# Norms of k from rounded high and low parts, and their place behind one output product

## The chip, the cores and the metric

The kernel runs on one core of one Trainium2 chip. The metric is the device time of one execution in microseconds; lower is better. The engines are PE (TensorE), DVE (VectorE), ACT (ScalarE), POOL (GpSimd) and SP, the queue that issues the DMAs.

## The reference

The input is x of 8 batch elements, 512 tokens and 256 channels, in float32. One attention layer with 16 heads and complex q, k and v (64 real and 64 imaginary parts a head) is followed by a small feed-forward layer; each has a normalisation before and after and a residual. The change is in the norms of k:

```python
qr = q * phase[None]
kr = k * phase[None]
s = jnp.einsum('bihd,bjhd->bhij', qr, jnp.conj(kr)).real
qn = (q.real ** 2 + q.imag ** 2).sum(-1).transpose(0, 2, 1)
kn = (k.real ** 2 + k.imag ** 2).sum(-1).transpose(0, 2, 1)
maha = jnp.maximum(qn[..., None] + (E * E)[None] * kn[:, :, None, :] - 2.0 * E[None] * s, 0.0) / V[None]
logits = coef * jnp.log1p(maha / nu[None, :, None, None]) - 0.5 * DH_ * jnp.log(V)[None]
A = jax.nn.softmax(logits, axis=-1)
y = jnp.concatenate([out.real.reshape(B_, N_, DKt), out.imag.reshape(B_, N_, DKt)], axis=-1)
return y @ Wo
```

## The kernel before

The 16 heads are taken in 8 groups of two, and within a group the 8 batch elements one after the other: 64 turns, t = 0 to 63. A turn handles the pair (group, element) c; at the same time it finishes the pair before (cp) and starts the next (cn). The order on every engine is written out by hand in a function `body`, one for each engine, and semaphores with fixed counts tie the engines together.

For the next pair a turn does this. PE projects q (z = 0) and k (z = 1) into the two PSUM banks pa0 (real parts) and pa1 (imaginary parts), in `project` (L767), from weights and x that are split into a rounded high part and a low part of type float32r. ACT squares each bank (`square`, L1182). DVE multiplies the banks with the cosine and the sine (`rotate`, L1508): four products RC, IS, RS and IC for q, and four for k. POOL adds the squares of the real and the imaginary parts (`sum_squares`, L584) and combines the rotated products into qk (`rotated`, L592). The norms of k are then matrix products of the sums with a matrix of ones (`norms_k`, L778, one product for each head, on 64 rows each, float32), written into pa0 and pa1. They may begin once the last `rotate` of k has read the banks (wait on mul_dve). ACT copies them with a bias into kn (`keep_norm_k`, L1188), and POOL makes ek from kn (`decay_norm`, L602). The norms of q (`norm_q`, L786) go into pa0 and wait for the first of these copies.

Scores are a product of qk (`scores`, L807), which DVE turns into lg in two steps (`decay`, L1622, and `distance`, L1632) and, after a logarithm on ACT (L1199), a third one (`logits`, L1639). After the exponential (L1207) PE transposes the probabilities (`turn`, L819) into pp0 or pp1, ACT copies them out (L1214), and `attend` (L831) multiplies them with the values. `values` (L797) writes pp0 and pp1 too, and ACT copies these into vt (`keep_values`, L1193). `keep_y` (L1220) copies the result of a head.

The output products of the pair before are four calls of `out_project` (L842) for each turn: head 0 half 0, head 0 half 1, head 1 half 0, head 1 half 1. Each fills the whole bank po with four matmul records, and before the next may begin DVE must have read po, in `add_output` (L1660, and L1658 in the first group). This is the wait at the head of `out_project`:

```python
if half == 0:
    pe.wait_ge(y_act, c[2] + hh + 1)
pe.wait_ge(acc_dve, c[4] + 2 * hh + half)
```

So the product of head 1 half 0 waits until both halves of head 0 are added. On PE the end of a turn is: `out_project` (0,1), `turn` (0,0), `norms_k`, `out_project` (1,0), `scores` (0,0) of the next pair, `norm_q`, `scores` (0,1), `out_project` (1,1), `turn` (0,1), `scores` (0,2). On DVE the same stretch is: the rotations RS and IC of k, `add_output` (0,1), `decay` (1,3), `distance` (1,3), `add_output` (1,0), `decay` (0,0) of the next pair.

Of the kernel before, what the change touches and what calls it, by code (L numbers as in the profile page):

```python
# [21 lines left out]
F32 = mybir.dt.float32  # L22
F32R = mybir.dt.float32r
I32 = mybir.dt.int32
ALU = mybir.AluOpType
ACT = mybir.ActivationFunctionType
# [6 lines left out]
B, N, D = 8, 512, 256  # L33
H, DH = 16, 64
DK = H * DH
HID = 768
P = 128
KT = D // P
NT = N // P
HH = 2  # L40
# [24 lines left out]
def build(nc, x_d, wq_d, wk_d, wv_d, wo_d, omega_d, raw_d, tau_d, wg_d, wu_d, wd_d, out_d):  # L65
    ctx = ExitStack()
    with ctx:
# [3 lines left out]
        def sem(name):  # L71
            return ctx.enter_context(nc.semaphore(name))
# [19 lines left out]
        sq = sb("sq", [P, 2, 2, N])  # L92
# [7 lines left out]
        hx = sb("hx", [P, 4, N], F32R)  # L100
# [4 lines left out]
        heads = sb("heads", [P, HH, P])  # L105
# [72 lines left out]
        pa = [bank("pa0"), bank("pa1")]  # L178
# [45 lines left out]
        x_out = [sem(f"x_out{i}") for i in range(XBUF)]  # L224
# [5 lines left out]
        nk_rdy = sem("nk_rdy")  # L230
        nq_rdy = sem("nq_rdy")
        v_rdy = sem("v_rdy")
# [2 lines left out]
        av_rdy = sem("av_rdy")  # L235
        o_rdy = sem("o_rdy")
        sq_act = sem("sq_act")
        kn_act = sem("kn_act")
        v_act = sem("v_act")
        ln_act = sem("ln_act")  # L240
# [10 lines left out]
        sum_pool = sem("sum_pool")  # L251
# [76 lines left out]
        def width(n):  # L328
            return (TILES[n] + 1) * P

        def at(n):

            o = sum(width(k) for k in range(n))
            return slice(o, o + width(n))

        PARTS = ((0, 0), (0, 1), (1, 0))

# [382 lines left out]
        def _(pe):  # L720
            credit(pe, (proj, 4), (nk_rdy, 1), (nq_rdy, 1), (v_rdy, 2), (s_rdy, 8), (tr_rdy, 8), (av_rdy, 8), (o_rdy, 4))
            mm = pe.matmul
# [46 lines left out]
                        n += 1  # L769
                last.then_inc(proj, 1)  # L770

            def norms_k(c):

                pe.wait_ge(sum_pool, c[2] + 2)
                pe.wait_ge(mul_dve, c[8] + 8)
                for hh in range(HH):
                    row = slice(hh * DH, (hh + 1) * DH)
                    last = mm(pa[hh][:, :], heads[row, hh, :], sq[row, 1, 0, :], start=True, stop=True)  # L778
                last.then_inc(nk_rdy, 1)

            def norm_q(c):
# [53 lines left out]
            def out_project(c, par, hh, half):  # L835
# [4 lines that stand above are left out]
                for jj in range(2):  # L840
                    j = 2 * half + jj
                    last = mm(po[:, jj * D:(jj + 1) * D], yt[:, hh, j * P:(j + 1) * P], wot[:, par, hh * D:(hh + 1) * D],  # L842
                              start=True, stop=True)
                last.then_inc(o_rdy, 1)
# [69 lines left out]
            def body(it):  # L914


                c = counts(pe, it.t, PERS)
                cp, cn = previous(c), following(c)
                old, nxt = it.before is not None, it.behind is not None
                half = it.half + it.slot  # L920
                if it.opens is not None:
                    pe.wait_ge(w_lo, 3 * KT * (it.opens + 1))
                    pe.wait_ge(wo_in[it.behind], 32 * (it.opens // 2 + 1))
                if nxt:
                    project(cn, it.behind, 1 - it.slot, it.xn, half, it.own, 0, 0)
                if it.own == 1:
                    ffn_turn(2)
                if old:
                    turn(cp, 0, 2)
                scores(c, 0, 3)  # L930
                if it.own is not None and it.own < B - 1:
                    x_turn(cp, it.own + 1, 0)
                if nxt:
                    project(cn, it.behind, 1 - it.slot, it.xn, half, it.own, 0, 1)
                if old:
                    attend(cp, 0, 0, 1 - it.slot)
                    attend(cp, 0, 1, 1 - it.slot)
                    turn(cp, 0, 3)
                scores(c, 1, 0)
                if it.own is not None and it.own < B - 1:  # L940
                    x_turn(cp, it.own + 1, 1)
                if old:
                    turn(cp, 1, 0)
                    attend(cp, 0, 2, 1 - it.slot)
                if nxt:
                    project(cn, it.behind, 1 - it.slot, it.xn, half, it.own, 1, 0)
                if it.own == 1:
                    ffn_turn(3)
                    ffn_turn(4)
                    ffn_turn(5)  # L950
                if old:
                    attend(cp, 0, 3, 1 - it.slot)
                scores(c, 1, 1)
                if old:
                    turn(cp, 1, 1)
                    turn(cp, 1, 2)
                    attend(cp, 1, 0, 1 - it.slot)
                scores(c, 1, 2)
                if old:
                    turn(cp, 1, 3)  # L960
                scores(c, 1, 3)
                if it.own is not None and it.own < B - 1:
                    pe.wait_ge(x_lo, 2 * it.own + 4)
                if old:
                    out_project(cp, it.before, 0, 0)
                if nxt:
                    project(cn, it.behind, 1 - it.slot, it.xn, half, it.own, 1, 1)
                else:
                    f_transposes(0)
                if it.own == 1:  # L970
                    ffn_turn(6)
                    ffn_turn(7)
                    ffn_turn(8)
                    pe.wait_ge(ffn_ev, 9)
                if old:
                    attend(cp, 1, 1, 1 - it.slot)
                    attend(cp, 1, 2, 1 - it.slot)
                values(c, it.par, it.x, 0)
                values(c, it.par, it.x, 1)
                if old:  # L980
                    attend(cp, 1, 3, 1 - it.slot)
                    out_project(cp, it.before, 0, 1)
                turn(c, 0, 0)
                if nxt:
                    norms_k(cn)
                if old:
                    out_project(cp, it.before, 1, 0)
                if nxt:
                    scores(cn, 0, 0)
                    norm_q(cn)  # L990
                    scores(cn, 0, 1)
                if old:
                    out_project(cp, it.before, 1, 1)
                turn(c, 0, 1)
                if nxt:
                    scores(cn, 0, 2)
                else:
                    gate_up(0, 0)
                    gate_up(0, 1)
# [49 lines left out]
            c = counts(pe, G * B - 1, PERS)  # L1049
# [40 lines left out]
        def _(act):  # L1090
# [10 lines left out]
            for h in range(HH):  # L1101
                for a in range(2):
                    row = slice(h * DH + a * DH // 2, h * DH + (a + 1) * DH // 2)
# [80 lines left out]
            def keep_norm_k(c, par, hh):  # L1184
# [2 lines left out]
                act.wait_ge(ek_pool, c[8] + 4 * hh + 4 - 8)  # L1187
                act.activation(kn[:, hh, :], pa[hh][:, :], ACT.Identity, bias=ncog[:, par, 1, hh:hh + 1]).then_inc(kn_act, 1)  # L1188

            def keep_values(c, slot, half):  # L1190

                act.wait_ge(v_rdy, c[2] + 1 + half)
                act.activation(vt[:, slot, 2 * half:2 * half + 2, :].rearrange("p a n -> p (a n)"), pp[half][:, :],  # L1193
                               ACT.Copy).then_inc(v_act, 1)
# [6 lines left out]
            def exp(c, hh, n):  # L1201
                m, q = 4 * hh + n, NT * hh + TILES[n]
                act.wait_ge(f_dve, c[8] + m + 1)
                act.wait_ge(tr_rdy, c[8] + m + 1 - 8)
                if n == 0:
                    act.wait_ge(rd_dve, c[2] + hh + 1 - 2)
                act.activation(pr[:, hh, at(n)], lg[:, hh, at(n)], ACT.Exp, bias=nmax[:, q:q + 1], scale=-1.0,  # L1207
                               accum_out=den[:, q:q + 1]).then_inc(ex_act, 1)
# [56 lines left out]
            def body(it):  # L1265
# [60 lines left out]
                if not nxt:  # L1326
                    f_high(0)
                exp(c, 0, 0)
                keep_values(c, it.slot, 0)
                if old:  # L1330
                    keep_y(cp, 1)
# [100 lines left out]
        def _(dve):  # L1432
# [69 lines left out]
            def rotate(c, par, z, m):  # L1502

                r = m in (IS, IC)
                dve.wait_ge(sq_act, c[4] + 2 * z + r + 1)
                for h in range(HH):
                    dve.wait_ge(rot_pool[h], c[4] + (1 + (m in (RS, IC)) if z else 0))
                tt(rm[:, m, :], pa[r][:, :], ropet(par, m in (IS, RS)), ALU.mult).then_inc(mul_dve, 1)  # L1508
# [126 lines left out]
            def logits(c, hh, n, par):  # L1635
# [3 lines left out]
                dve.tensor_tensor_reduce(lg[:, hh, at(n)], lg[:, hh, at(n)], tab(par, hh, T3_T, w), ncog[:, par, 0, hh:hh + 1],  # L1639
                                         3e38, ALU.add, ALU.min, nmax[:, q:q + 1]).then_inc(f_dve, 1)  # L1640

            def inverse(c, hh):

                dve.wait_ge(ex_act, c[8] + 4 * hh + 4)
                rec(rden[:, NT * hh:NT * hh + NT], den[:, NT * hh:NT * hh + NT]).then_inc(rd_dve, 1)
# [111 lines left out]
            def body(it):  # L1757
# [69 lines left out]
                if nxt:  # L1827
                    rotate(cn, it.behind, 1, RS)
                    rotate(cn, it.behind, 1, IC)
                if old:  # L1830
                    add_output(cp, it.b_before, it.over, 0, 1)
                if nxt:
# [117 lines left out]
```

## Time and profile before

| | |
|---|---|
| median of 3 runs | 1871.65 us (1870.67 to 1872.46) |
| the profiled execution | 1871.72 us, of which the span from the first to the last instruction is 1869.9 us |
| mean granted TensorE clock | 0.991 |
| PE busy | 1795.5 us, 96% of the span |
| DVE, ACT, POOL busy | 87%, 84%, 79% |
| DMA | mean 63 GB/s |

Busy time is the time in which an engine had an instruction in flight, as a share of the span. Matmuls are pipelined: a matmul's row tells when it began and how long it was in flight, and the next one often begins while it still runs. What a group of matmuls takes from PE is therefore read from its start to the start of the next group.

### The profile page before, as it was taken

The page shows a single profiled execution, that of the slowest core. Times are in us where ns is not written, and L with a number is a line of the kernel's source. Part 1 is how long each engine was busy: PE and PEld are TensorE (multiplying, and loading weights), DVE is VectorE, ACT ScalarE, POOL GpSimd, SP SyncE. Part 2 cuts the span into 40 slices and gives each one's busy share as a digit, 9 for nine tenths or more (in the row PEclk, how much of TensorE's full clock was granted, in tenths as well). Part 3 has the DMA queues.
Part 4 walks back from the last instruction along what each step waited for, and adds up shares of the span by engine and source line. Part 5 has one row for each costly group of instructions (what it writes and reads, how often), then busy time and mean ns, then how long its engine had stood idle before and what let it go on. Part 6 is the DMA issues. An engine that isn't in the chain of part 4 may idle for free.

```text
span 1869.9 us, 35435 instructions
## 1 busy us (share of the span) xinstructions
PE 1795.5 (96%) x10690; PEld 1475.9 (79%) x10690; DVE 1631.4 (87%) x3852; ACT 1576.7 (84%) x3255; POOL 1470.0 (79%) x1291
## 2 busy tenths in 40 slices
PE   5799999999999999999999999999999999988997
PEld 3577788878888888778888888788888888867876
DVE  7799989989888899988898899888898888986885
ACT  5798888898888888998888888988888888876654
POOL 5677888878888888888888888888888888862664
PEclk9899999999999999999999999999999999999999
DMA  6311211131112201131203111120112111010111
GB/s 184 118 68 46 85 46 68 45 104 46 63 52 68 86 26 67 46 125 46 68 30 101 46 63 52 63 98 33 69 46 91 46 46 45 25 57 13 46 46 45
DMA packets 61100, 117.77 MB, mean 63 GB/s; under 512 B 13504, under 2 KB 42944, under 8 KB 52720
## 3 DMA queue, kind: packets, MB, share of 16 engines
q1 hardware_dynamic: 60528, 115.51, 18.4%
q8 instruction: 88, 1.44, 0.3%
q14 instruction: 100, 0.82, 0.2%
q10 hardware_dynamic: 384, 0.00, 0.0%
HBM read 99.64 MB, written 21.36 MB: 65 GB/s over the span
## 4 chain that ended last, share of the span: by engine, by line
PE 70%; DVE 11%; ACT 4%; issue 3%; POOL 2%; DMA 0%; DVEq 0%; POOLq 0%; ACTq 0%; SPq 0%
PE pa L767 15%; PE py L831 13%; PE ps L807 12%; PE po L842 10%; PE pp L797 8%; PE pp L819 6%; PE pa L778 3%; PE pa L786 2%; DVE lg L1639 2%; DVE stats L1666 1%; DVE rm L1508 1%; DVE lg L1632 1%; DVE acc L1688 1%; DVE ps L1622 1%; DVE tabs L1753 1%
## 5 line engine op out<-in xcount | busy, mean ns | idle before, releaser
L592 POOL TENSOR_TENSOR qk<-rm 64x512 f32<-64x512 f32 x504 | 697.4, 1384 | 93.7 <-PE ps L807 49.8
L602 POOL TENSOR_TENSOR ek<-tabs,kn 128x512 f32<-128x512 f32 (+3 forms) x512 | 463.7, 911 | 133.9 <-DVE lg L1632 107.0
L1639 DVE CUSTOM_DVE_ANT_0 lg<-lg,tabs,ncog 128x512 f32<-128x512 f32 (+3 forms) x512 | 445.5, 888 | 0.0
L767 PE MATMUL pa<-xt,wt 128*128 128x512 f32 x1488 | 420.8, 418 | 6.3 <-DVE rm L1514 3.7
L1508 DVE TENSOR_TENSOR rm<-pa,tabs 128x512 f32<-128x512 f32 x504 | 327.0, 676 | 75.1 <-POOL qk L592 66.1
L807 PE MATMUL ps<-qk 128*128 128x512 f32 (+3 forms) x1024 | 366.9, 443 | 12.0 <-DVE lg L1632 11.8
L831 PE MATMUL py<-pt,vt 128*128 128x128 f32 x2560 | 348.2, 275 | 0.8 <-ACT pt L1214 0.5
L1632 DVE CUSTOM_DVE_ANT_0 lg<-ps,ek,qb 128x512 f32<-128x512 f32 (+3 forms) x512 | 279.0, 545 | 76.1 <-issue 58.0
L831 PEld LDWEIGHTS py<-pt,vt 128*128 128x128 f32 x2560 | 331.1, 192 | 16.8 <-ACT pt L1214 0.7
L767 PEld LDWEIGHTS pa<-xt,wt 128*128 128x128 f32 x1488 | 273.5, 191 | 58.7 <-issue 7.9
L1199 ACT ACTIVATE lg<-lg,qb 128x512 f32<-128x512 f32 (+3 forms) x512 | 273.0, 557 | 17.4 <-DVE lg L1632 13.5
L1207 ACT ACTIVATE pr<-lg,nmax 128x512 f32<-128x512 f32 (+3 forms) x512 | 283.7, 555 | 1.5
L842 PE MATMUL po<-wot,yt 128*128 128x256 f32 x1024 | 270.4, 387 | 3.0 <-DVE acc L1660 3.0
L1214 ACT ACTIVATE pt<-pp 128x512 f32<-128x512 f32 (+3 forms) x512 | 219.8, 429 | 59.5 <-PE pp L819 42.9
L1622 DVE TENSOR_TENSOR ps<-ps,tabs 128x512 f32<-128x512 f32 (+3 forms) x512 | 249.3, 487 | 17.8 <-PE ps L807 17.6
L842 PEld LDWEIGHTS po<-wot,yt 128*128 128x128 f32 x1024 | 179.1, 190 | 81.2 <-issue 48.4
L819 PEld LDWEIGHTS pp<-ident,pr 128*128 128x128 f32 x1280 | 162.9, 141 | 92.9 <-issue 58.4
L819 PE MATMUL pp<-ident,pr 128*128 128x128 f32 x1280 | 214.3, 274 | 15.4 <-ACT pt L1214 12.8
L1660 DVE SCALAR_TENSOR_TENSOR acc<-po,rden,acc 128x256 f32<-128x256 f32 x480 | 207.6, 472 | 10.0 <-PE po L842 9.6
L1182 ACT ACTIVATE sq<-pa 128x512 f32<-128x512 f32 x256 | 151.9, 594 | 60.8 <-PE pa L767 60.6
L797 PE MATMUL pp<-wt,xt 128*128 128x256 f32 x1488 | 193.6, 286 | 0.7 <-ACT wut L1162 0.7
L584 POOL TENSOR_TENSOR sq<-sq 128x512 f32<-128x512 f32 x126 | 161.8, 1284 | 39.9 <-ACT sq L1182 39.3
(205 smaller groups left out, 2251.5 us busy)
## 6 DMA issues: line engine op xcount, KB each, us to landing
xt<-xs_d SPq DMA_DIRECT2D x56, 1024.0 KB, 4.8
tabs<-vec_d SPq DMA_DIRECT2D x7, 1536.0 KB, 6.5
xs_d<-xt SPq DMA_DIRECT2D x6, 1024.0 KB, 4.3
wt<-wraw_d SPq DMA_DIRECT2D x7, 768.0 KB, 6.7
acc<-in_L_attn_x SPq DMA_DIRECT2D x8, 512.0 KB, 6.2
tabs<-in_L_attn_x SPq DMA_DIRECT2D x8, 512.0 KB, 4.8
tabs<-rope_d SPq DMA_DIRECT2D x56, 64.0 KB, 5.8
out<-tabs SPq DMA_DIRECT2D x7, 512.0 KB, 3.2
```

The costliest lines, as they stand in the source:

```text
L592: pool.tensor_tensor(qk[part * DH:(part + 1) * DH, z * HH + hh, :], rm[row, 2 * part, :], rm[row, 2 * part + 1, :], ALU.add if part else A ...
L602: pool.tensor_tensor(ek[:, n % 2, 0:w], tab(par, hh, E2_T, w), kn[:, hh, 0:w], ALU.mult).then_inc(ek_pool, 1)
L767: last = mm(pa[r][:, :], wproj(par, z, kt, a, r * P, (r + 1) * P), xbuf[x][:, kt, b, :], start=(n == 0), stop=(n == 3 * KT - 1))
L797: last = mm(pp[half][:, jj * W2:(jj + 1) * W2], xbuf[x][:, kt, a, j * P:(j + 1) * P], wproj(par, 2, kt, b, 0, W2), start=(n == 0), stop=(n ...
L807: mm(ps[n % 2][:, 0:w], qk[:, hh, TILES[n] * P:(TILES[n] + 1) * P], qk[:, HH + hh, 0:w], start=True, stop=True).then_inc(s_rdy, 1)
L819: last = pe.transpose(pp[i][:, j * P:(j + 1) * P], pr[:, hh, o:o + P], ident[:, :])
L831: last = mm(py[:, I * P:(I + 1) * P], vt[:, slot, j, hh * P:(hh + 1) * P], pt[:, i, j * P:(j + 1) * P], start=(j == 0), stop=(j == I))
L842: last = mm(po[:, jj * D:(jj + 1) * D], yt[:, hh, j * P:(j + 1) * P], wot[:, par, hh * D:(hh + 1) * D], start=True, stop=True)
L1207: act.activation(pr[:, hh, at(n)], lg[:, hh, at(n)], ACT.Exp, bias=nmax[:, q:q + 1], scale=-1.0, accum_out=den[:, q:q + 1]).then_inc(ex_ac ...
L1508: tt(rm[:, m, :], pa[r][:, :], ropet(par, m in (IS, RS)), ALU.mult).then_inc(mul_dve, 1)
L1632: dve._custom_dve(bass.dve_ops.TENSOR_ADD_SAT, out=lg[:, hh, at(n)], in0=ps[n % 2][:, 0:w], in1=ek[:, n % 2, 0:w], s0=3e38, s1=qb[:, slot, ...
L1639: dve.tensor_tensor_reduce(lg[:, hh, at(n)], lg[:, hh, at(n)], tab(par, hh, T3_T, w), ncog[:, par, 0, hh:hh + 1], 3e38, ALU.add, ALU.min, ...
```

## The change

The norms of k are computed in another way for every pair from the second group on (t of the pair at least 8, 56 of the 63 calls in the turns). ACT writes a copy of the sums of squares, rounded to float32r, into the buffer hx (`high_sum`); DVE subtracts it from the sums to give the low part (`low_sum`); and PE makes four float32r products, high and low part for each head, in place of two float32 products. hx was a buffer for x in the first group and is free afterwards. The matrix of ones is copied once into hx as float32r. The copy on ACT stands between `exp` (0,0) and `keep_values` of half 0; the subtraction on DVE between the rotation IC of k and `add_output` (0,1). On PE `norms_k` moves behind `out_project` (1,0), in all turns, those of the first group too.

```diff
+        def parted(t):
+            return B <= t
+        def k_sums(a):
+            return hx[:, a, :]
+        round_heads = hx[:, 2, 0:HH * P].rearrange("p (h n) -> p h n", h=HH)
...
-            def norms_k(c):
+            def norms_k(c, t):
                 pe.wait_ge(sum_pool, c[2] + 2)
                 pe.wait_ge(mul_dve, c[8] + 8)
-                for hh in range(HH):
-                    row = slice(hh * DH, (hh + 1) * DH)
-                    last = mm(pa[hh][:, :], heads[row, hh, :], sq[row, 1, 0, :], start=True, stop=True)
+                if parted(t):
+                    pe.wait_ge(nl_dve, t - B + 1)
+                    for a in range(2):
+                        for hh in range(HH):
+                            row = slice(hh * DH, (hh + 1) * DH)
+                            last = mm(pa[hh][:, :], round_heads[row, hh, :], hx[row, a, :], start=(a == 0), stop=(a == 1))
+                else:
+                    for hh in range(HH):
+                        row = slice(hh * DH, (hh + 1) * DH)
+                        last = mm(pa[hh][:, :], heads[row, hh, :], sq[row, 1, 0, :], start=True, stop=True)
                 last.then_inc(nk_rdy, 1)
...
                 turn(c, 0, 0)
-                if nxt:
-                    norms_k(cn)
                 if old:
                     out_project(cp, it.before, 1, 0)
+                if nxt:
+                    norms_k(cn, it.t + 1)
                 if nxt:
                     scores(cn, 0, 0)
                     norm_q(cn)
...
+            def high_sum(t):
+                act.wait_ge(sum_pool, 2 * t + 4)
+                if t == B:
+                    act.wait_ge(v_rdy, 2 * (B - 2) + 2)
+                    act.wait_ge(x_out[2], 16 * 2)
+                    act.activation(round_heads, heads[:, :, :], ACT.Copy)
+                else:
+                    act.wait_ge(nk_rdy, t + 1)
+                act.activation(k_sums(0), sq[:, 1, 0, :], ACT.Copy).then_inc(nh_act, 1)
...
                 exp(c, 0, 0)
+                if nxt and parted(it.t + 1):
+                    high_sum(it.t + 1)
                 keep_values(c, it.slot, 0)
...
+            def low_sum(t):
+                dve.wait_ge(nh_act, t - B + 1)
+                tt(k_sums(1), sq[:, 1, 0, :], k_sums(0).bitcast(F32), ALU.subtract).then_inc(nl_dve, 1)
...
                 if nxt:
                     rotate(cn, it.behind, 1, RS)
                     rotate(cn, it.behind, 1, IC)
+                if nxt and parted(it.t + 1):
+                    low_sum(it.t + 1)
                 if old:
                     add_output(cp, it.b_before, it.over, 0, 1)
```

## Rows read from the trace of the kernel before

**Rows 1.** Two turns by engine: busy us (instructions) on each engine, clock.

```profile
core 0: us, PE busy (x) PEld busy (x) DVE busy (x) ACT busy (x) POOL busy (x), PEclk, DMA share, GB/s
270.87:295.97 25.10, 25.07 (x152) 20.76 (x153) 22.41 (x53) 22.12 (x47) 20.96 (x18) 1.00 0.12 41
905.68:930.78 25.10, 25.07 (x152) 20.77 (x153) 22.43 (x53) 22.44 (x48) 21.53 (x20) 1.00 0.22 74
```

**Rows 2.** Timeline of a middle turn: start, us, engine, line, tiles [idle before, releaser].

```profile
922.60 0.39 PE L807 MATMUL ps<-qk 128*128 128x128 f32 x2
...
923.16 2.65 POOL L592 TENSOR_TENSOR qk<-rm 64x512 f32<-64x512 f32 x2 [0.77 <-PE ps L807]
...
924.56 0.69 DVE L1508 TENSOR_TENSOR rm<-pa,tabs 128x512 f32<-128x512 f32 x1 [1.27 <-POOL qk L592]
...
927.39 3.18 POOL L592 TENSOR_TENSOR qk<-rm 64x512 f32<-64x512 f32 x2
...
927.88 1.54 DVE L1639 CUSTOM_DVE_ANT_0 lg<-lg,tabs,ncog 128x384 f32<-128x384 f32 x1
...
928.98 0.58 ACT L1193 ACTIVATE vt<-pp 128x512 f32<-128x512 f32 x1
...
929.36 1.28 DVE L1508 TENSOR_TENSOR rm<-pa,tabs 128x512 f32<-128x512 f32 x2
...
930.16 0.60 PE L819 MATMUL pp<-ident,pr 128*128 128x128 f32 x4
...
930.56 0.86 DVE L1660 SCALAR_TENSOR_TENSOR acc<-po,rden,acc 128x256 f32<-128x256 f32 x2
...
930.78 1.26 POOL L592 TENSOR_TENSOR qk<-rm 64x512 f32<-64x512 f32 x1 [0.21 <-DVE rm L1508]
930.78 1.13 PE L778 MATMUL pa<-sq,heads 64*128 64x512 f32 x4
...
931.84 1.13 PE L842 MATMUL po<-wot,yt 128*128 128x256 f32 x4
931.95 0.69 ACT L1188 ACTIVATE kn<-pa,ncog 128x512 f32<-128x512 f32 x1 [0.78 <-PE pa L778]
...
932.81 1.02 PE L807 MATMUL ps<-qk 128*128 128x512 f32 x2
...
933.67 0.95 PE L786 MATMUL pa<-heads,sq 128*128 128x2 f32 x8
...
936.40 0.58 ACT L1214 ACTIVATE pt<-pp 128x512 f32<-128x512 f32 x1
...
937.99 0.37 PEld L819 LDWEIGHTS pp<-ident,pr 128*128 128x128 f32 x2
...
938.57 1.64 PE L767 MATMUL pa<-xt,wt 128*128 128x512 f32 x6
...
940.05 1.72 PE L831 MATMUL py<-pt,vt 128*128 128x128 f32 x14
```

**Rows 3.** Timelines of PE and DVE in turn 0, an early and a late turn.

```profile
73.13 1.13 PE L807 MATMUL ps<-qk 128*128 128x512 f32 x2
...
74.09 0.50 PE L786 MATMUL pa<-heads,sq 128*128 128x2 f32 x4
...
191.60 1.28 DVE L1508 TENSOR_TENSOR rm<-pa,tabs 128x512 f32<-128x512 f32 x2
...
193.03 1.13 PE L778 MATMUL pa<-sq,heads 64*128 64x512 f32 x4 [0.46 <-DVE rm L1508]
...
1610.65 1.28 DVE L1508 TENSOR_TENSOR rm<-pa,tabs 128x512 f32<-128x512 f32 x2
...
1612.08 1.13 PE L778 MATMUL pa<-sq,heads 64*128 64x512 f32 x4
```

**Rows 4.** Groups of like instructions: count, busy us, mean ns of one, idle before.

```profile
L1721 DVE TENSOR_TENSOR tabs<-tabs,acc 128x1024 f32<-128x1024 f32 x7 | 8.8, 1260 | 1.6 <-ACT tabs L1259 1.6
L1251 ACT ACTIVATE wt<-tabs 128x512 fp32r<-128x512 f32 x36 | 22.7, 630 | 37.2 <-DVE tabs L1753 34.0 <-PE po L893 3.2
```

More of the change, by code:

```diff
@@ L237, in build @@
         sq_act = sem("sq_act")
+        nh_act = sem("nh_act")
+        nl_dve = sem("nl_dve")
         kn_act = sem("kn_act")
```

## The prediction

> **What bounds the kernel now.** I read the table of busy time by stage first, then the timeline of a middle turn on all engines, then the same place in other turns. The table shows a turn of 25.10 us in which PE is busy for 25.07 [rows 1]. The easy reading is that PE is the bound and that every microsecond of matmul removed is gained. But busy counts a matmul that is in flight, also over a short stall, and the timeline says more. The next thing to look at is what ends just before `norms_k` starts. DVE's last two rotations of k (RS, IC) run from 929.36 to 930.64, and `norms_k` begins at 930.78, 0.14 us later, while the four transposes before it, from 930.16, are in flight for 0.60 in all, so that the last has left by 930.76 and PE could take the next product at about 930.60 [rows 2]. An early turn has 191.60 + 1.28 = 192.88 and 193.03, 0.15 later, with the wait for the rotation named; a late one has 1611.93 and 1612.08, again 0.15 [rows 3]. A distance that doesn't move over the whole kernel is a wait, not a coincidence. So PE is held here by DVE, for at most 0.2 us a turn, and the loop that sets the turn is: `scores` (1,3) on PE at 922.60, POOL's rotated products that may start only after it (0.77 us idle, released by L807), DVE's rotation RC that may start only after those (1.27 us idle, released by POOL), DVE without a gap until IC ends at 930.64, then `norms_k`, and from there PE without a gap until the next `scores` (1,3) [rows 2]. In this loop PE has up to 0.2 us of slack on the way to `norms_k`, and DVE has none.
>
> **The change, part by part.** Times are those of the middle turn [rows 2].
>
> *The move on PE.* Today `norms_k` (930.78 to 931.84, 1.06 us) stands between `turn` (0,0) and `out_project` (1,0). That product waits for `add_output` (0,1), since all four output products share the bank po. The addition ends at 930.56 + 0.86 = 931.42, under `norms_k`: its cover costs nothing today. Moved behind the product, `norms_k` no longer covers it. PE would be free at 930.60 and wait.
>
> *The subtraction on DVE.* `low_sum` stands ahead of just this addition. A rotation of the same 512 columns takes 0.60 us from start to start (929.36, 930.56, two of them). Its inputs are both in SBUF; the nearest such row is the addition of 1024 columns at 1260 ns [rows 4], half of it 0.63. I take 0.61. It goes ahead of the addition in DVE's order, so the addition ends at 931.42 + 0.61 = 932.03. From the end on DVE to the start on PE I take the 0.14 of IC to `norms_k`: `out_project` (1,0) starts at 932.17 in place of 931.84, 0.33 later. Bounds: the subtraction can't be free, since its place is on the loop; the hand-over could be 0.05 to 0.2.
>
> *The norms as rounded products.* Their cost isn't in the trace. Before: four records of 64 rows, 1.06 us together. After: four float32r matmuls of 64 rows and 512 columns. A float32r matmul of 512 columns and 128 rows goes at (940.05 - 938.57)/6 = 0.247 us [rows 2]. If the two heads run side by side on their halves of the rows, as the float32 ones do (four records in 1.06 us, while two records of full height and 512 columns, `scores`, take 0.86), the four take 2 x 0.25 and 0.05 for the change of shape, 0.55. If they run one after the other, 4 x 0.25 = 1.0. I take 0.55; nothing in the program separates the two cases other than the type. Before them I allow 0.05.
>
> *What follows.* `out_project` itself takes 932.81 - 931.84 = 0.97. So `scores` (0,0) starts at 932.17 + 0.97 + 0.05 + 0.55 = 933.74 in place of 932.81, 0.93 later. Then `norm_q`, which waits for ACT's copy of the first head's norms. That copy starts today 0.11 after the next product on PE (931.95) and takes 0.69, and `scores` (0,0) needs 0.86: after the move it is the only cover. Turn 0 has just this order, and there `scores` to `norm_q` is 74.09 - 73.13 = 0.96 [rows 3], 0.10 more than the 0.86. Sum of a turn: +1.03 us.
>
> *The copy on ACT.* `high_sum` costs about 0.60 (a copy to float32r of 512 columns has 630 ns [rows 4]). It pushes `keep_values` from 928.98 to 929.6, ending 930.2, so `turn` (0,0) starts perhaps 0.1 late; that lies under PE's new wait until 932.17. If that wait weren't there it would cost about 0.1 a turn. Further on, ACT's copy of the norms comes at about 933.9 in place of 931.95, 1.9 later, where PE is 1.03 later. The copy L1214 at 936.40 then ends near 938.9 and PE's transposes need it at 937.99 + 1.03 = 939.0. That just fits, so I put nothing for it, and up to 0.2 a turn for the upper end. POOL's rotated product at 930.78 comes behind `low_sum` and moves by some 0.4; the bit of ek for (1,3) behind it isn't waited for by PE in this stretch.
>
> *The port.* Rows show that a DVE instruction that reads two tiles of SBUF stands still while POOL works: `logits` on 384 columns takes 1.54 us from 927.88, with POOL's products running from 927.39 to 930.57 at 1.59 each, so the first of them ends at about 929.0, and 929.0 + 0.4 is where DVE ends [rows 2]. The Trainium skill has the rule in "SBUF — State Buffer", section "Who interferes with whom": two SBUF inputs on DVE and a GpSimd instruction that reads SBUF exclude each other, and whoever issues first keeps the port for the whole instruction. By that rule the trace agrees. For the sum it matters who is first: `low_sum` would start at 930.56, when POOL's products have just ended (930.57), and the next one starts at 930.78, 0.22 behind. So DVE is first and POOL waits.
>
> *The first group.* In turns 1 to 6 only the order changes: the addition ends at 931.42, the product starts at 931.56, `norms_k` at 932.58 with its old 1.06, `scores` at 933.64, +0.83, and +0.10 for `norm_q`: 0.93.
>
> *The sum.* 56 turns x 1.03 = 57.7, 6 x 0.93 = 5.6, together 63. Nothing gives it back: after `scores` (0,0) PE runs without a gap to `scores` (1,3), and the chain by POOL and DVE hangs on that one. The profiled execution's own 1871.72 + 63.3 = 1935.0; it lies 0.07 from the median, so this stands for the median as well.
>
> **Rivals.**
> 1. *The chain holds, sizes at the low end.* Hand-over 0.05, no allowance before the norms, nothing for `norm_q`, order of 0.75 a turn: 42 + 4.5, 1918. If `low_sum` were hidden too (DVE finding the time in an earlier wait) the product would start at 931.56 and the turn would be +0.43: 24 + 5 = 29, 1901. Against it: there is no DVE wait between 924.56 and 930.64.
> 2. *The rounded products don't run side by side.* +0.45 a turn, 25 more: 1960. For it: no 64-row float32r matmul is in the trace.
> 3. *`low_sum` loses the port to POOL.* If POOL's product started first, DVE would stand for most of its 1.26 us: about +1.1 a turn, 62 more, 1997. It decides at 0.2 us between the two starts. The page "SBUF — State Buffer" would allow this outcome as well, since by its rule issue order alone decides.
> 4. *PE was the bound after all (the other side).* If the addition were ready when PE has finished `turn` (0,0), the whole saving of 1.06 - 0.55 = 0.5 would come through: 56 x 0.5 = 28, 1843. For this DVE's chain would have to run 1.4 us earlier against PE (932.03 against 930.60). Only 0.77 and 1.27 us of waits lie in it, and both hang on PE's own `scores` (1,3), so they don't give way. For it speaks only the busy share of PE.
> 5. *No difference*: needs the stalls to be just half as large as read, with no mechanism behind it.
>
> **How the numbers follow.** The forecast 1935 has 0.60, its own range 1915 to 1955; rival 1 in its lower part 0.10; rival 2 with 0.13; rival 3 with 0.05; rival 4 with 0.08; rival 5 with 0.04. The range for 8 in 10 takes in the lower case of rival 1 in good part and rival 2: 1908 to 1965. About 0.2% (3.7 us) is what this measurement can tell from no change. Slower 0.89, same 0.03, faster 0.08.
>
> **What the profile after would show.** PE idle before the first matmul of `out_project` (1,0), about 1.3 us a turn, released by the addition on DVE; that addition starting 0.6 us later after IC than before; the turn at about 26.1 us; the norms' four records in 0.55 us (right) or 1.0 (rival 2); `low_sum` at 0.6 us (right) or near 1.7 (rival 3); and `norm_q` 0.9 to 1.0 us behind the start of `scores` (0,0). The forecast is wrong if the additions come at the same time after `scores` (1,3) as before with `low_sum` in front of them, or if PE shows no wait at this place.

## The result

The changed kernel takes 1951.49 us (median; before 1871.16 in the same runs), a ratio of 1.0431 with the 95% interval [1.0418, 1.0443]. That is 80 us more; the forecast was 63 more, 1935, and its range ended at 1965. The profiled execution has a span of 1948.5 us, 78.6 more than before. One of the ten executions of e5 below took 9955 us and is left out of its ratio; the executions of every other kernel lie within 0.6% of each other.

First the page of the changed kernel, its busy times and its chain:

```profile
PE 1794.6 (92%) x10690; PEld 1463.7 (75%) x10690; DVE 1668.3 (86%) x3908; ACT 1590.0 (82%) x3312; POOL 1487.2 (76%) x1291
...
PE 44%; DVE 29%; issue 7%; POOL 5%; ACT 4%; DVEq 1%; POOLq 0%; DMA 0%; ACTq 0%; SPq 0%
```

PE's busy time hardly moved (1795.5 before, 1794.6 now), though the norms' matmuls now take 0.66 us to the next product and not 1.06: busy counts what is in flight, so a short wait behind a matmul that is still in flight is in it. What changed is the share, 96% before and 92% now, and the chain, in which DVE now has 29% where it had 11%. The table of busy time by stage, for a plain turn and for two turns in which ACT also computes sines for a rotation table (they are named below):

```profile
core 0: us, PE busy (x) PEld busy (x) DVE busy (x) ACT busy (x) POOL busy (x), PEclk, DMA share, GB/s
918.59:944.89 26.30, 24.98 (x154) 20.51 (x154) 23.00 (x54) 22.45 (x47) 21.27 (x18) 1.00 0.11 40
410.62:439.42 28.80, 25.37 (x153) 20.42 (x153) 22.77 (x54) 25.07 (x51) 21.78 (x19) 1.00 0.52 164
1234.56:1265.38 30.82, 27.17 (x155) 21.78 (x154) 23.66 (x54) 25.19 (x51) 21.61 (x19) 0.94 0.11 37
```

A plain turn went from 25.10 [rows 1] to 26.30, and PE, which was without a gap, is idle for 1.3 of it. DVE rose by the subtraction, 0.6. The timeline of that turn, at the same place as [rows 2], shows where:

```profile
934.29 0.39 PE L824 MATMUL ps<-qk 128*128 128x128 f32 x2
...
940.67 0.61 ACT L1216 ACTIVATE hx<-sq 128x512 fp32r<-128x512 f32 x1
...
941.04 1.28 DVE L1538 TENSOR_TENSOR rm<-pa,tabs 128x512 f32<-128x512 f32 x2
...
942.25 0.68 DVE L1675 TENSOR_TENSOR hx<-sq,hx 128x512 fp32r<-128x512 f32 x1
942.47 1.58 POOL L602 TENSOR_TENSOR qk<-rm 64x512 f32<-64x512 f32 x1 [0.23 <-DVE rm L1538]
...
942.85 0.86 DVE L1695 SCALAR_TENSOR_TENSOR acc<-po,rden,acc 128x256 f32<-128x256 f32 x2
...
943.86 1.10 PE L859 MATMUL po<-wot,yt 128*128 128x256 f32 x4 [1.32 <-DVE acc L1695]
...
944.89 0.73 PE L791 MATMUL pa<-hx 64*128 64x512 f32 x4
...
945.55 1.13 PE L824 MATMUL ps<-qk 128*128 128x512 f32 x2
...
945.66 0.69 ACT L1205 ACTIVATE kn<-pa,ncog 128x512 f32<-128x512 f32 x1 [2.33 <-PE pa L791]
...
946.51 1.01 PE L803 MATMUL pa<-heads,sq 128*128 128x2 f32 x8
...
947.38 0.89 PE L824 MATMUL ps<-qk 128*128 128x384 f32 x2
```

Read it from the bracket: the product L859 stood for 1.32 us, released by the addition L1695. The addition ends at 942.85 + 0.86 = 943.71 and the product starts 0.15 later. Ahead of the addition stands the subtraction L1675, 0.60 from its start to the next. Counted from the last `scores` of head 1 (L807 at 922.60 before, L824 at 934.29 now), the rotations start 6.76 and 6.75 later, so DVE's chain to this point didn't move at all. The product starts 9.24 and 9.57 later (+0.33), the first scores 10.21 and 11.26 (+1.05), `norm_q` 11.07 and 12.22 (+1.15), and the next scores 11.88 and 13.09 (934.48 and 947.38, +1.21). That is the whole loss of a plain turn.

Over the kernel, from the starts of the norms in both traces: 48 plain turns from the second group on lost 58.9 us, 1.23 each; the six turns with sines 15.6; the first group 4.0; the two last turns 0.2. Together 78.7.

### The profile page after: what moved, and what is told of

Read it like the earlier page. It is cut to its first block, busy times and chain, and to the rows that moved or that the text cites. A ratio compares the mean times of both kernels' runs of the same rounds, so it can differ in the third digit from the quotient of the medians.

```text
span 1948.5 us, 35604 instructions
## 1 busy us (share of the span) xinstructions
PE 1794.6 (92%) x10690; PEld 1463.7 (75%) x10690; DVE 1668.3 (86%) x3908; ACT 1590.0 (82%) x3312; POOL 1487.2 (76%) x1291
## 4 chain that ended last, share of the span: by engine, by line
PE 44%; DVE 29%; issue 7%; POOL 5%; ACT 4%; DVEq 1%; POOLq 0%; DMA 0%; ACTq 0%; SPq 0%
PE ps L824 11%; PE pa L777 10%; DVE lg L1669 9%; PE py L848 8%; PE po L859 5%; DVE rm L1538 5%; DVE acc L1695 5%; POOL qk L602 4%; PE pp L836 4%; DVE lg L1662 3%; PE pa L803 2%; PE pa L791 2%; DVE ps L1652 1%; DVE stats L1701 1%; DVE acc L1723 1%
## 5 line engine op out<-in xcount | busy, mean ns | idle before, releaser
L602 POOL TENSOR_TENSOR qk<-rm 64x512 f32<-64x512 f32 x504 | 715.0, 1419 | 89.8 <-PE ps L824 45.6
L1669 DVE CUSTOM_DVE_ANT_0 lg<-lg,tabs,ncog 128x512 f32<-128x512 f32 (+3 forms) x512 | 450.8, 898 | 0.1
L777 PE MATMUL pa<-xt,wt 128*128 128x512 f32 x1488 | 422.7, 420 | 6.4 <-DVE rm L1544 3.7
L824 PE MATMUL ps<-qk 128*128 128x512 f32 (+3 forms) x1024 | 373.6, 450 | 9.3 <-DVE lg L1662 9.0
L859 PE MATMUL po<-wot,yt 128*128 128x256 f32 x1024 | 270.0, 387 | 84.3 <-DVE acc L1695 75.9
L777 PEld LDWEIGHTS pa<-xt,wt 128*128 128x128 f32 x1488 | 274.9, 192 | 58.8 <-issue 8.0
L859 PEld LDWEIGHTS po<-wot,yt 128*128 128x128 f32 x1024 | 180.7, 192 | 128.3 <-issue 96.0
L1242 ACT ACTIVATE pt<-pp 128x512 f32<-128x512 f32 (+3 forms) x512 | 219.6, 429 | 52.7 <-PE pp L836 43.8
L836 PEld LDWEIGHTS pp<-ident,pr 128*128 128x128 f32 x1280 | 158.2, 141 | 108.1 <-issue 79.7
L1695 DVE SCALAR_TENSOR_TENSOR acc<-po,rden,acc 128x256 f32<-128x256 f32 x480 | 207.9, 473 | 10.7 <-PE po L859 10.6
L1205 ACT ACTIVATE kn<-pa,ncog 128x512 f32<-128x512 f32 x128 | 87.1, 681 | 149.3 <-PE pa L791 131.8
```

Source lines behind the costliest of these rows:

```text
L602: pool.tensor_tensor(qk[part * DH:(part + 1) * DH, z * HH + hh, :], rm[row, 2 * part, :], rm[row, 2 * part + 1, :], ALU.add if part else A ...
L777: last = mm(pa[r][:, :], wproj(par, z, kt, a, r * P, (r + 1) * P), xbuf[x][:, kt, b, :], start=(n == 0), stop=(n == 3 * KT - 1))
L824: mm(ps[n % 2][:, 0:w], qk[:, hh, TILES[n] * P:(TILES[n] + 1) * P], qk[:, HH + hh, 0:w], start=True, stop=True).then_inc(s_rdy, 1)
L836: last = pe.transpose(pp[i][:, j * P:(j + 1) * P], pr[:, hh, o:o + P], ident[:, :])
L1695: last = stt(dst, po[:, jj * D:(jj + 1) * D], rden[:, NT * hh + j:NT * hh + j + 1], dst, ALU.mult, ALU.add)
```

## The experiments

Every run was taken beside runs of the kernel before on the same chip (medians 1871.2 to 1871.9). Each edit is against the kernel named with it.

**e1: the move alone, on the kernel before.**

```diff
                 turn(c, 0, 0)
-                if nxt:
-                    norms_k(cn)
                 if old:
                     out_project(cp, it.before, 1, 0)
+                if nxt:
+                    norms_k(cn)
```

> The kernel before with one edit: norms_k, float32 as before, stands behind the output product of head 1 half 0. No copy, no subtraction, no rounded products. Theory 'lost cover' (the slowdown comes from the place of norms_k): the addition ends 0.78 us after the last rotation, the output product starts 0.15 later, 0.27 earlier than now; product to norms 1.03, norms to scores 1.19 as in turn 0, norm_q another 0.16 late: +1.14 us in a plain turn, some 65 to 72 in all, 1937 to 1944. The move alone costs nearly what the whole change costs. Rival 'added work' (subtraction and copy cost it): no more than the first group's few us, 1873 to 1882.

Measured: 1943.05 us, ratio 1.0376 [1.0353, 1.0400]. Moving one call costs 71 of the 80 us. In its timeline the product is what waits:

```profile
936.78 0.86 DVE L1660 SCALAR_TENSOR_TENSOR acc<-po,rden,acc 128x256 f32<-128x256 f32 x2
...
937.79 1.10 PE L842 MATMUL po<-wot,yt 128*128 128x256 f32 x4 [0.82 <-DVE acc L1660]
938.82 1.13 PE L778 MATMUL pa<-sq,heads 64*128 64x512 f32 x4
...
939.88 1.13 PE L807 MATMUL ps<-qk 128*128 128x512 f32 x2
```

A plain turn is 26.12 here, +1.02 where 1.14 was expected: the norms took 1.06 us from start to start, as in the middle turns before, and not the 1.19 of turn 0. The theory of the lost cover stands, that of the added work falls. But that the median lies in the range expected is in part luck: the traced execution is the shortest of the four, 1934.97 us at a mean granted clock of 0.990, and its 63 us more are what the waits of the timeline make. The other three took 1942.3 to 1945.4 us at 0.984 to 0.987; no trace shows where in them the clock was lower. So some 8 of the 71 us stand only in executions with a lower clock.

**e2: the changed kernel with `norms_k` back in its old place** (the same lines the other way round; copy, subtraction and rounded products stay).

> The changed kernel with norms_k put back ahead of the output product of head 1 half 0; copy, subtraction and rounded products stay. Theory 'lost cover': the norms start 0.60 later (they wait for the subtraction), take 0.66, and the output product waits for its addition until 1.53 us after the last rotation in place of 1.20: +0.33 us a turn, about 18 to 25 in all, 1889 to 1896. Rival 'added work': near the changed kernel's 1951. A third possibility, that the cheaper norms pay at once: below 1871.

Measured: 1888.59 us, 1.0093 [1.0078, 1.0108], 17 more than before. Its plain turn is 25.40:

```profile
912.53 0.67 DVE L1675 TENSOR_TENSOR hx<-sq,hx 128x512 fp32r<-128x512 f32 x1
...
913.36 0.73 PE L791 MATMUL pa<-hx 64*128 64x512 f32 x4 [0.53 <-DVE hx L1675]
...
914.14 1.10 PE L859 MATMUL po<-wot,yt 128*128 128x256 f32 x4
```

Now the norms wait for the subtraction, 0.53 us. So undoing the move takes 63 us off, as expected, but the rest of the change is no gain in this order either: what PE saves is spent waiting for the operation that makes the saving possible.

**e3: the changed kernel with the subtraction behind the addition on DVE.**

```diff
                     rotate(cn, it.behind, 1, IC)
-                if nxt and parted(it.t + 1):
-                    low_sum(it.t + 1)
                 if old:
                     add_output(cp, it.b_before, it.over, 0, 1)
+                if nxt and parted(it.t + 1):
+                    low_sum(it.t + 1)
```

> The changed kernel with the subtraction behind the addition of head 0 half 1 on DVE, so that the addition is not delayed by it. All else as changed. Theory: the output product starts 0.60 us earlier than in the changed kernel, and the norms still don't wait for the subtraction: 0.60 a turn less, 34 us less in all, 1915 to 1920. Rival (the place of the subtraction does not matter because DVE has waits that take it up): 1951 as changed.

Measured: 1928.26 us, 1.0306 [1.0290, 1.0321]: 23 less than changed, not 34. The plain turn fell by 0.46 to 25.85. The six turns with sines gained nothing (16.0 us over the kernel before, 15.6 in the changed one; the granted clock fell in four of them). Why a plain turn fell by less than 0.60 the timeline says:

```profile
908.56 0.86 DVE L1695 SCALAR_TENSOR_TENSOR acc<-po,rden,acc 128x256 f32<-128x256 f32 x2
908.78 1.26 POOL L602 TENSOR_TENSOR qk<-rm 64x512 f32<-64x512 f32 x1 [0.22 <-DVE rm L1538]
...
909.34 1.25 DVE L1675 TENSOR_TENSOR hx<-sq,hx 128x512 fp32r<-128x512 f32 x1
...
909.57 1.10 PE L859 MATMUL po<-wot,yt 128*128 128x256 f32 x4 [0.73 <-DVE acc L1695]
...
910.74 0.73 PE L791 MATMUL pa<-hx 64*128 64x512 f32 x4
```

The product starts 0.93 us after the last rotation, as expected. But the subtraction takes 1.25 us and not 0.67: POOL's product runs from 908.78 to 910.04, the subtraction was issued in the middle of it, and ends 0.55 after it. The norms then follow the subtraction (910.59) by 0.15. In the changed kernel it is the other way round: the subtraction is first by 0.22 us and takes 0.68, and POOL's product behind it is stretched from 1.26 to 1.58. The norms start 1.17 us after the product where it is 1.03 in the changed kernel; these 0.14 are just what the turn of 25.85 has over the 25.71 expected. This is the rule that the prediction took from the Trainium skill, "SBUF — State Buffer", section "Who interferes with whom" (whoever issues first keeps the port), and both orders of it agree with it here: the second of the two was held each time, by 0.58 us on DVE (1.25 for 0.67) and by 0.32 on POOL.

**e12: the changed kernel without the subtraction.** It leaves the low part of the sums out of the norms of k and adds the product of the high part twice.

```diff
-                    pe.wait_ge(nl_dve, t - B + 1)
+                    pe.wait_ge(nh_act, t - B + 1)
...
-                            last = mm(pa[hh][:, :], round_heads[row, hh, :], hx[row, a, :], start=(a == 0), stop=(a == 1))
+                            last = mm(pa[hh][:, :], round_heads[row, hh, :], hx[row, 0, :], start=(a == 0), stop=(a == 1))
...
-                if nxt and parted(it.t + 1):
-                    low_sum(it.t + 1)
```

> The changed kernel with the same cut (no subtraction on DVE, the product of the high part twice). Theory (the subtraction costs its own 0.60 us in each of the 56 turns, because it stands ahead of the addition that the output product waits for): 26.31 falls to 25.71, 34 us less, 1915 to 1920. Rival (e3 took only 23 us off by moving it; if that was the share of the subtraction and not the port): 1926 to 1930.

Measured: 1918.26 us, 1.0250 [1.0231, 1.0268], 33 less than the changed kernel. The norms start at 882.51 and 908.23: a turn of 25.72. The wait of the product fell to the rest, 0.72:

```profile
882.51 0.73 PE L791 MATMUL pa<-hx 64*128 64x512 f32 x4
908.23 0.74 PE L791 MATMUL pa<-hx 64*128 64x512 f32 x4
...
932.91 1.10 PE L859 MATMUL po<-wot,yt 128*128 128x256 f32 x4 [0.72 <-DVE acc L1695]
```

So the subtraction costs its own length, 0.59 us in a plain turn, and what was missing in the plain turn of e3 was the port.

**e4: the kernel before, `logits` (1,1) out of the way of the last two rotations.** It tests the claim of the prediction that DVE, and not PE, held the turn by some 0.2 us.

```diff
-                logits(c, 1, 1, it.par)
                 if not nxt:
+                    logits(c, 1, 1, it.par)
                     logits(c, 1, 2, it.par)
...
                     add_output(cp, it.b_before, it.over, 0, 1)
                 if nxt:
+                    logits(c, 1, 1, it.par)
                     decay(c, 1, 3, it.par)
```

> The kernel before with one edit on DVE: logits of (1,1), 1.54 us ahead of the last two rotations of k, is moved behind the addition of head 0 half 1. No part of the change is in it. Theory (DVE's chain holds PE at norms_k for some 0.2 us a turn, and PE's own work is the next bound right behind it): 0.1 to 0.2 us a turn less, 8 to 12 in all, 1860 to 1864. Rival (PE alone is the bound): 1870 to 1873. If the moved logits only delay the distance step and the next addition: above 1873.

Measured: 1868.39 us, 0.9982 [0.9973, 0.9991]. All plain turns are now 25.01, where before they were 25.10 with some of 25.28. DVE did hold PE, but by 0.09 us in most turns: from the first transposes to the norms it is 0.53 us here (902.94 and 903.47) and 0.62 before (930.16 and 930.78) [rows 2], so the rest of the 0.2 isn't a wait for DVE. The saving expected, 8 to 12 us, was about three times too large: the 48 plain turns gave 5.4 back, and three turns of the first group became 2.1 longer together. In the middle turns PE shows no wait any more: its own work is the bound there.

**e6: the changed kernel with the edit of e4.**

> The changed kernel with the same edit on DVE as in e4 (logits of (1,1) behind the addition of head 0 half 1). Theory: the last rotation ends some 1.3 us earlier against PE, but the subtraction then waits for ACT's copy and for POOL, as in e5 where it ended 1.8 us after the last rotation, so the addition and the output product come only about 0.35 us earlier against PE: 0.3 to 0.4 us a turn less than the changed kernel, 1929 to 1935. Rival (the wait at the output product is not made by DVE's order): 1951.

Measured: 1938.33 us, 1.0358 [1.0341, 1.0376]. The plain turn fell from 26.31 to 25.98, as expected; in all it was 13 us, 3 short of the range expected, since the six turns with sines and the first group gained nothing together (14.9 and 4.7 us over the kernel before, 15.6 and 4.0 in the changed one). The granted clock fell in three of the six turns here, in two of them in the changed kernel.

**e5: e2 with the edit of e4.**

> The order of e2 (norms ahead of the output product, with copy, subtraction and rounded products), and DVE's third step of the scores, logits of (1,1), 1.54 us in the way of the last two rotations, is moved behind the addition of head 0 half 1. Theory: the loop through DVE sets the turn, so with 1.5 us less ahead of the last rotation PE stops waiting and the cheaper norms show: 0.3 to 0.6 us a turn less than before, 1840 to 1855. Rival (PE's own work or ACT is the next bound at once): 1865 to 1872. If moving the logits only pushes the wait to the next place on DVE (distance, add_output): above 1871.

Measured: 1874.81 us, 1.0013 [1.0003, 1.0023], a turn of 25.08. The forecast failed. Counted from the last `scores` of head 1, DVE's last rotation ends 1.5 us earlier (6.53 us behind it and not 8.04), but the subtraction starts only with ACT's copy, and POOL then holds it (a rotated product of POOL runs from 904.09 to 905.35):

```profile
903.97 0.61 ACT L1216 ACTIVATE hx<-sq 128x512 fp32r<-128x512 f32 x1
...
904.62 1.29 DVE L1675 TENSOR_TENSOR hx<-sq,hx 128x512 fp32r<-128x512 f32 x1 [0.49 <-ACT hx L1216]
...
906.05 0.74 PE L791 MATMUL pa<-hx 64*128 64x512 f32 x4 [0.21 <-DVE hx L1675]
```

**e7: the changed kernel with the sines behind ACT's other work of the turn** (and **e8**: the kernel before with this edit and that of e4).

```diff
-                elif it.rope is not None and it.rope[1] == 3:
-                    rope_sines(it.rope[0])
-                elif it.rope is not None and it.rope[1] == 4:
-                    rope_cosine(it.rope[0])
                 if nxt:
                     log(c, 1, 3, it.slot)
                 keep_turned(c, 0, 0)
...
                     log(cn, 0, 1, 1 - it.slot)
+                if it.rope is not None and it.rope[1] == 3:
+                    rope_sines(it.rope[0])
+                elif it.rope is not None and it.rope[1] == 4:
+                    rope_cosine(it.rope[0])
```

> The changed kernel, with the sines and cosines of the rotation tables (ACT, six turns in all) moved from ahead of the log of (1,3) to the end of the turn's list, behind the log of (0,1). It tests why these six turns lost 2.0 to 4.1 us where a plain turn lost 1.2: theory, ACT's list behind the copies of the norms came later against PE, and PE stood 2.1 us before the third transposes (1.3 before), long enough for the clock to fall to half twice. With the sines out of this way that wait goes and the clock stays up: 6 to 15 us less, 1937 to 1945. Rival (the loss in these turns has another cause, or the moved sines hold the squares instead): 1949 to 1955.

> The kernel before with both edits, of e4 and of e7, without any part of the change: the candidate to beat both kernels. Theory: e4's gain and the 1.6 us of each of the six turns with sines (26.7 against 25.1), up to 9: 1852 to 1858. Rival (the moved sines hold the squares of the next turn by as much): 1860 to 1866.

Measured: e7 1953.85 us, 1.0441 [1.0425, 1.0456]; e8 1877.05, 1.0028 [1.0017, 1.0039], slower than e4 by 9. All six turns are 30.2 in e7 (28.7 to 30.8 changed) and 28.1 in e8. The moved sines hold the copies of the transposes in the next turn: PE stands for 0.70 and 1.84 us there, released by L1242. The clock stayed up in e7, but that gave back less than the new waits took. Neither theory's time came. The old place of the sines was the better one, and the edit doesn't tell what the six turns lost; the traces do, with e1 and e2, below.

**e9: room for the rounded products, and e10: the same order without them.** Against e5, the product of head 0 half 1 is issued between the two calls of `values`, and its addition stands ahead of the subtraction, both behind the last rotation. e10 has the same order with the float32 norms and no copy or subtraction.

```diff
                 values(c, it.par, it.x, 0)
+                if old:
+                    out_project(cp, it.before, 0, 1)
                 values(c, it.par, it.x, 1)
                 if old:
                     attend(cp, 1, 3, 1 - it.slot)
-                    out_project(cp, it.before, 0, 1)
```

> The copy, the subtraction and the rounded products of the change, norms_k ahead of the output product of head 1 half 0 as before, and room made for them: the output product of head 0 half 1 stands between the two calls of values on PE, its addition on DVE right behind the last rotation, then the subtraction, then logits of (1,1). Theory (the cheaper norms are worth 0.4 us a turn of PE work once neither the addition nor the subtraction is late): 24.6 to 24.8 us a plain turn, 1845 to 1858. Rival (DVE, ACT or POOL is the bound by then, or ACT's copy holds the subtraction): a turn of 25.0 to 25.1, 1866 to 1876. If POOL holds the port for the subtraction: above that.

> The same order as e9 without any part of the change: norms_k as one float32 product for each head, no copy, no subtraction. Theory (PE's own work is 25.01 us a turn with these norms, as e4 has it): 25.0 us a turn, 1865 to 1870, so that the difference to e9 is what the rounded products themselves are worth.

Measured: e9 1867.51 us, 0.9979 [0.9969, 0.9989]; e10 1864.65, 0.9960 [0.9948, 0.9973]. Both beat the kernel before, by 0.2% and 0.4%, and the one without the change is the faster. For e9 the rival's time came and not the theory's. e10 has turns of 24.99 with PE busy without a gap. e9 has 24.98, and its timeline again shows the subtraction held by POOL, 1.07 us (the second of the three products merged in the first row runs from 898.97 to 900.25), and PE waiting for it:

```profile
897.28 4.66 POOL L602 TENSOR_TENSOR qk<-rm 64x512 f32<-64x512 f32 x3
...
899.73 1.07 DVE L1676 TENSOR_TENSOR hx<-sq,hx 128x512 fp32r<-128x512 f32 x1
...
900.95 0.73 PE L791 MATMUL pa<-hx 64*128 64x512 f32 x4 [0.21 <-DVE hx L1676]
```

**e11: e9 without the subtraction** (the same cut as in e12: the low part of the sums is left out, the high product added twice).

> e9 with DVE's subtraction left out: this kernel leaves the low part of the sums out of the norms of k and adds the product of the high part twice, so PE does the same four rounded products and waits for ACT's copy only. Theory (in e9 the subtraction, held 0.45 us by POOL's use of the port, keeps PE waiting before the norms, and that wait eats what the cheaper norms save): the turn falls from 24.98 to 24.6 to 24.75, 1845 to 1855. Rival (another engine or PE's own work is the bound at 24.98): 1864 to 1868.

Measured: 1853.77 us, 0.9905 [0.9890, 0.9920], 14 less than e9, a turn of 24.70, with no wait at the norms:

```profile
894.81 0.74 PE L791 MATMUL pa<-hx 64*128 64x512 f32 x4
```

So the rounded products are worth 0.29 us in most plain turns against e10 once nothing is late, in all 11 us. It is the subtraction, at every place tried, that eats them.

## Why the prediction was right, and where it was off

**What bounds the kernel.** Right: the busy share of PE misled, and the loop through POOL and DVE ended just at the norms. e4, with nothing of the change in it, shows DVE's hold on PE, but at 0.09 us for most turns, under the 0.2 that the prediction allowed at most.

**The move.** Right, and the main part: e1 has 71 of the 80 us, 63 of them in the execution without the lower clock. The product waits for the addition as soon as the norms no longer lie between.

**The subtraction.** Right in place and size: 0.61 taken, 0.60 measured in the start of the addition, 0.59 a turn in e12. The hand-over from DVE to PE is 0.15 where 0.14 was taken, and the product starts 0.33 later, as forecast.

**The norms.** The heads do run side by side (two pairs within 0.73 us in flight; rival 2 falls). But from their start to the next product is 0.66 where the sum had 0.55, 0.11 too little: each pair takes 0.33, where the sum had 0.25 for a pair, after the matmuls of 128 rows, and 0.05 once for the change of shape.

**What follows.** `norm_q` starts 0.96 after the scores, as forecast. The row behind it wasn't in the sum: the eight small products take 0.87 where they took 0.81, 0.06; no run shows why. With 0.11 and 0.01 elsewhere this is 0.18 of a plain turn, 48 turns, 9 us of the 17 missing.

**The copy on ACT.** Here a step failed for six turns. The prediction found that ACT's copy of the transposes "just fits" and put nothing for it. It did in plain turns. In two turns of three of the groups ACT has a table load and two functions more (sines in one, cosines in the next) in just that list, and there PE was already waiting for L1214 before: 1.21 to 1.32 us. This is one of them in the kernel before and the same place after:

```profile
1190.94 0.41 PE L819 MATMUL pp<-ident,pr 128*128 128x128 f32 x2 [1.22 <-ACT pt L1214]
```

```profile
1242.97 0.41 PE L836 MATMUL pp<-ident,pr 128*128 128x128 f32 x2 [2.02 <-ACT pt L1242]
1243.22 0.55 PE L824 MATMUL ps<-qk 128*128 128x128 f32 x2
1243.42 2.91 PE L777 MATMUL pa<-xt,wt 128*128 128x512 f32 x6
```

ACT's copy of the norms comes 2.0 us later and PE only 1.2, so PE waits 0.8 longer, and four of these turns lost 2.0 in all. It is the move that does it, and not `high_sum`: e1, with the move alone, waits 2.02 to 2.12 us at these six places, and e2, with `high_sum` but the norms in their old place, 1.11 to 1.20.

```profile
388.77 0.41 PE L819 MATMUL pp<-ident,pr 128*128 128x128 f32 x2 [2.03 <-ACT pt L1214]
```

```profile
381.58 0.41 PE L836 MATMUL pp<-ident,pr 128*128 128x128 f32 x2 [1.11 <-ACT pt L1242]
```

The first is from e1, whose six turns take 28.5 to 28.6 us, the second from e2, where they take 26.9 to 27.0 (26.7 to 26.8 before). In the other two of the six turns of the changed kernel the clock fell as well:

```profile
1239.30:1243.30 4.00, 1.98 (x11) 1.38 (x10) 2.22 (x7) 3.96 (x7) 3.05 (x3) 1.00 0.00 0
1243.30:1246.70 3.40, 3.40 (x12) 2.82 (x12) 1.61 (x5) 2.54 (x7) 0.73 (x1) 0.50 0.00 0
```

PE was busy for 1.98 of 4.00 us, and then the granted clock is 0.50 for 3.4 us (the lower level, 1.2 GHz); the six matmuls of L777 are in flight for 2.91, and for 1.63 at the same place of a turn in which the clock stayed up (390.67). The two turns lost 4.1 and 3.4 us. The six turns make 15.6 us, 8 more than six times a plain turn. The longer wait is shown by e1 and e2; what the lower clock adds is read from the traces alone, since e7, meant to test it, only moved the wait.

**The first group.** 5.6 forecast, 4.0 measured over the whole stretch; e1 has 3.4 there. In three of the turns, of 28.5 to 29.1 us, the move cost nothing to speak of, since PE already waited some 0.4 us ahead of the norms (0.46 in the turn of [rows 3]), and the product now takes that place.

**Rivals.** Rival 1 fell on its sizes: the hand-over is 0.15 and not 0.05, `norm_q` did cost its 0.10, and DVE found no earlier wait for `low_sum`. Rival 4 (the saving comes through) failed because neither of the waits in DVE's chain gave way: DVE's rotations start at the same distance from `scores` (1,3) to 0.01 us. Rival 5 (no difference) fell with the result. Rival 3 (POOL first at the port) wasn't this kernel's case, but it is what happened in e3, e5 and e9.

**Luck.** A little of it is in the forecast: in the traces the sum is too small by 9.6 us for the plain turns and by 9.4 for the six with sines, but too large by 1.6 for the first group and by 1.8 for the two last turns, which lost 0.2 in place of 2.

## What to carry to other kernels

When an engine is busy for almost all of a stage (here 25.07 of 25.10 us), look at what ends just before each of its instructions: work that seems to cost a microsecond may be covering a wait, and moving it away brings the wait out in full. Before a product is made cheaper by splitting its input, place the operation that does the split: here it takes DVE 0.60 us, more than the 0.40 us that it saves PE, and it stood on the same loop. A DVE instruction with two inputs in SBUF is best placed where POOL is idle: a product of POOL that had started first took it from 0.67 to 1.25 us here.

## What the hardware showed beyond that

- Matmuls of 64 rows on the two halves of the array start together (within 0.04 us) in float32 and in float32r. Two pairs take 1.06 us to the next product in float32 and 0.66 in float32r, 62% of it.
- A subtraction of 512 columns with both inputs in SBUF took 0.67 to 0.68 us where it started first, 1.07, 1.25 and 1.29 where a product of POOL had, and a POOL product behind it took 1.58 for 1.26.
- PE waits of 2.02 us at the same place in two turns (390.28 and 1242.97) were followed by the lower clock in one and not in the other, in the same execution. In the traced execution of e1 the six such waits (2.02 to 2.12 us) were followed by it in none, in that of e3 (2.02 to 2.13) in four.
